# Graph attention on Trainium2: one of ten scaled one-hot copies moved from ScalarE into a fused VectorE maximum

## The reference, cut to what matters

```python
h = x @ Wn.T + bn
e = edge_attr @ We.T + be
a = leaky_relu(sum((h[src] + e) * attn, axis=-1), 0.01)
m = segment_max(a, dst, num_segments=N)
a = exp(a - m[dst])
denom = segment_sum(a, dst, num_segments=N)
out = relu(segment_sum(h[src] * (a / (denom[dst] + 1e-16))[..., None], dst, num_segments=N))
```

## Time and profile before

| | |
|---|---|
| median of three runs | 3936.38 us (3935.75 to 3937.24) |
| the profiled execution | 3933.78 us, its span 3932.0 us |
| busy over the span | PE 80%, PEld 59%, DVE 61%, ACT 46%, POOL 31% |
| granted clock, mean of the span | 0.919 |
| mean DMA rate | 167 GB/s |

### The profile page before, as it was taken

The page is one execution under the profiler, slowest core; times in us unless marked ns, Lnnn a source line. Parts: engine busy times, 40 slices in busy tenths (PEclk is TensorE's granted clock), DMA queues, the critical chain, the costliest instruction groups (busy, mean ns, idle before and its releaser), DMA issues. The chain is left out here.

```text
span 3932.0 us, 83459 instructions
## 1 busy us (share of the span) xinstructions
PE 3146.6 (80%) x17737; PEld 2338.0 (59%) x17738; DVE 2408.5 (61%) x6494; ACT 1816.4 (46%) x6302; POOL 1227.2 (31%) x988
## 2 busy tenths in 40 slices
PE   5666666998887776989944445898999899999978
PEld 4444445887876665767733335787888444445455
DVE  7999998987876565234467777777766400001754
ACT  1888883344445552011189985777776000000111
POOL 1688888888888810111000000000000000002512
PEclk9999999999998898999955558999999999999989
DMA  2444444677788884767576654434332643541067
GB/s 98 127 121 122 120 123 109 182 223 222 239 243 267 270 287 152 226 201 212 167 222 213 206 177 131 144 120 127 108 102 70 204 131 120 185 155 56 0 222 260
DMA packets 438469, 654.85 MB, mean 167 GB/s; under 512 B 102637, under 2 KB 293742, under 8 KB 438244
## 3 DMA queue, kind: packets, MB, share of 16 engines
q1 hardware_dynamic: 351298, 519.69, 42.5%
q10 hardware_dynamic: 56434, 125.33, 8.9%
q0 software_dynamic: 30640, 8.64, 3.1%
HBM read 436.96 MB, written 215.57 MB: 166 GB/s over the span
## 5 line engine op out<-in xcount | busy, mean ns | idle before, releaser
L1076 POOL DMA_INDIRECT slots<-all_B,put_index x800 | 1039.2, 1299 | 341.6 <-issue 335.5
L2354 PE MATMUL gio_po<-gio_T,all_A 125*128 125x500 f32 (+1 forms) x1400 | 530.9, 541 | 5.8 <-DMA gio_T<-pair 5.8
L2354 PEld LDWEIGHTS gio_po<-gio_T,all_A 125*128 125x128 f32 x1400 | 250.2, 190 | 283.3 <-issue 276.7
L1047 PE MATMUL put_ps<-put_right_in,put_left_in 128*128 128x125 f32 x2210 | 318.7, 294 | 65.8 <-ACT put_left_in L904 65.3
L2101 PE MATMUL att_ps<-att_right,att_left 128*125 128x125 f32 x2380 | 312.9, 285 | 70.0 <-ACT att_right L2122 56.6
L1337 ACT ACTIVATE lm_raised<-lm_hot,srt_words 128x125 f32<-128x125 bf16 x1200 | 350.9, 385 | 35.8 <-DVE srt_words L1237 24.8
L1655 PE MATMUL c_po<-c_halves,c_T 125*125 125x512 f32 x1250 | 327.7, 411 | 19.7 <-DVE c_halves L1747 10.0
L1371 PE MATMUL lm_ps<-lm_v,lm_node 125*128 x1220 | 170.5, 184 | 215.5 <-issue 79.2
L2101 PEld LDWEIGHTS att_ps<-att_right,att_left 128*125 128x125 f32 x2380 | 284.7, 191 | 94.2 <-issue 84.7
L1047 PEld LDWEIGHTS put_ps<-put_right_in,put_left_in 128*128 128x128 f32 x2210 | 281.0, 202 | 89.8 <-ACT put_left_in L904 75.6
L2175 DVE SCALAR_TENSOR_TENSOR att_power<-soft_negated,srt_words,att_far 128x125 f32 (+1 forms) x1190 | 320.1, 344 | 3.7 <-ACT att_right L2122 3.3
(11 more groups left out here) (441 smaller groups left out, 5245.3 us busy)
## 6 DMA issues: line engine op xcount, KB each, us to landing
c_T<-counts SPq DMA_DIRECT2D x255, 312.5 KB, 3.4
pair<-put_T ACTq DMA_DIRECT2D x125, 625.0 KB
att_ring<-hot SPq DMA_DIRECT2D x480, 160.0 KB
gio_T<-pair SPq DMA_DIRECT2D x60, 1250.0 KB, 5.8
hot<-put_hot SPq DMA_DIRECT2D x448, 160.0 KB
all_A<-in_edge_attr_dram SPq DMA_DIRECT2D x100, 448.0 KB
lm_planes<-src_rows SPq DMA_DIRECT2D x123, 320.0 KB, 3.9
counts<-put_T ACTq DMA_DIRECT2D x125, 312.5 KB
```

What stands on the lines that cost most here:

```text
L1047: ins = t_.matmul(tile(1, c), left_in[:, c, :], right_in[:, c, :], start=False, stop=False, skip_group_check=True)
L1076: nc.gpsimd.indirect_dma_start(slots, bass.IndirectOffsetOnAxis(index[:, C * g + j:C * g + j + 1], 0), stage[:, C * g + j, :], None).then_ ...
L2354: ins = t_.matmul(po[:, i % 2, h, 0:w], A[:, b, 128 * h:128 * h + 128], tiles, start=(b == 0), stop=(b == NB - 1))
```

## The change

ScalarE makes nine copies instead of ten. The halving becomes two VectorE instructions: a maximum over four pairs of copies (500 columns), and one `scalar_tensor_tensor` that multiplies the tenth one-hot, read from the ring `hot`, by its logit and takes the maximum with the fifth copy (125 columns). As VectorE now reads `hot`, SyncE waits for `grouped >= g+1` before it loads the ring's next slot. Apart from that, VectorE's block loop reads the two bounds of a block with one load of two registers (`Bounds`), where two loads of one register stood.

```diff
+class Bounds:
+    def __init__(self, eng, nc, s, k, name):
+        self.eng, self.nc, self.table = eng, nc, k["group_start"]
+        self.regs = s.registers(eng, name)
+
+    def at(self, d, n=0):
+        regs = self.regs[2 * n:2 * n + 2]
+        self.eng.load(regs, self.table[0:1, ds(d, 2)])
+        first, past = (self.eng.snap(r, donate=True) for r in regs)
+        return self.nc.s_assert_within(first, 0, NG - 1), self.nc.s_assert_within(past, 1, NG)
...
                         sp.wait_ge(lifted, g + 1)
                         sp.sem_inc(passed, 1)
+                        sp.wait_ge(grouped, g + 1)
+                        sp.sem_inc(passed, 1)
                         if not last or j < 3:
                             load_hot(g + 1, j + 1)
                         sp.wait_ge(hot_landed[j], 32 * i + 32)
...
-                    v.tensor_tensor((top if first else pairs)[:, :], lift[:, 0:G // 2 * P], lift[:, G // 2 * P:G * P], ALU.max
-                                    ).then_inc(grouped, 1)
+                    into, q = (top if first else pairs)[:, :], G // 2 - 1
+                    v.tensor_tensor(into[:, 0:q * P], lift[:, 0:q * P], lift[:, (q + 1) * P:(G - 1) * P], ALU.max)
+                    v.scalar_tensor_tensor(into[:, q * P:q * P + P],
+                                           hot[:, ds(g % RING, 1), :].rearrange("p a n -> p (a n)")[:, (G - 1) * S:(G - 1) * S + P],
+                                           logit[:, ds(G * g + G - 1, 1)], lift[:, q * P:q * P + P], ALU.mult, ALU.max
+                                           ).then_inc(grouped, 1)
...
+                bounds = Bounds(dve, nc, s, k, "bound")
                 with dve.Fori(0, NB) as d:
-                    g0, g1 = group_range(dve, k, d)
+                    g0, g1 = bounds.at(d)
...
-                        for c in range(G):
+                        for c in range(G - 1):
                             ins = nc.scalar.activation(raised[:, j % 2, c * P:(c + 1) * P], hot[:, j, c * S:c * S + P], ACT.Copy,
                                                        scale=logit[:, ds(G * g + c, 1)])
```

## The result

The changed kernel takes **3967.55 us** (median of four runs, 3965.67 to 3974.66) against 3936.07 (median of four, 3931.81 to 3937.24): ratio 1.008, 95% interval 1.0065 to 1.0095, **+31.5 us**. The prediction had the direction, half of the size (+14), and an upper end (3966) that the median passes by 1.5 us.

A forecast was written before the change was run, and what follows sets the result against it. It took ScalarE's copies to bound the 379 us stretch, the round through VectorE close behind. SyncE's later release (+15 us) and the block changes (-1) gave +14 on the median 3936.4, so 3950.4 us; range 3932 to 3966.

The forecast's parts named there:

- `grouped` after the halving's start: On VectorE, with the halving split in two instructions, `grouped` was to come 0.94 us after the halving starts, 0.13 later.
- SyncE's road: From the halving's end through SyncE's wait, loads and transfers to ScalarE's copy: 1.96 to 2.05 us, against 1.56 through the logits.
- ScalarE's idle time: Expected to rise to some 60 us, put down to SyncE's increment of `hot_arrived` in nearly every group, not to the logits.
- the prediction's own signs: What would show it right, among them ScalarE's busy time falling by 35 us while the stretch grows from 379 to some 393.
- Landings: Arrival of SyncE's one-hot transfers: 3.4 us free against a median landing of 2.5; late ones could add 0 to 4 us.
- SyncE's own turn allows it: SyncE's time from one pair of transfers to the next, 2.89 us, was held to fit under the new 3.02 a group.
- `Bounds` was mis-sized: One load of both bounds on VectorE was to save 0 to 0.52 us per change of block, taken as 0.35.
- the other round: Of two interleaved rounds of groups, a block change costs one 1.18 us, the other 0.77, as nine copies can catch up.
- The rest of the program does not touch the changed lines, so the whole argument lies in these 379 us: Only the stretch from 1976 to 2355 us, where ScalarE's copies run, was considered; no term covered later stages.
- Rival 1: SyncE's added wait costs nothing and the logits' round rules: -17 us, so 3919 us; chance 13%.
- the changes of block: At 24 places where VectorE starts a new block, 0.35 us each was to be saved: 8 us if the wait cost nothing.
- The slack of 0.04: Over two groups, ScalarE's own 5.80 us and the round through VectorE, 5.76, were only 0.04 us apart.

## Why the prediction was right in direction and half in size

**The mechanism holds.** ScalarE had no slack, the added wait put the release of group g behind halving g-2, and what stands behind the wait on SyncE decides: two instructions more behind it gave +8.3 us (6.2 more than the same two in front of it), one transfer fewer -26.6, the wait for the right group -23.8, and the wait alone was enough for +30.9. Single terms:

- `grouped` after the halving's start: predicted 0.94, measured 0.940 (0.811 before). The halving of 500 columns takes 0.680, 0.13 less; the fused instruction 0.344, as in the earlier trace rows; the overlap is 0.08. The rule for fp32 `tensor_tensor` that the prediction weighed (the Trainium skill, VectorE: DVE Perf Modes, "The TRN2 errata") gives an estimate of 0.678 for 500 columns, and the trace agrees with 0.680. Taken for the 125 columns of the fused operation the estimate would be 0.29, and the trace has 0.344; the sum with the measured row was the better one.
- SyncE's road: first transfer 0.84 predicted, 0.83 to 0.86 where SyncE came in time; pair 0.85; the copy 0.25 to 0.36 behind it. Where SyncE is in time this is the 1.96 to 2.05 of the prediction.
- ScalarE's idle time was expected at some 60 us and put down to SyncE; it is 87, and for all but one group it is SyncE's. The 60 didn't fit the prediction's own signs: 35 us less busy in a stage 14 us longer make 49 more, on top of the 36 of before. Measured are 28 less busy (a run of copies that ends in idle time shows its last copy in full, so not every copy saved is 0.29) and 23 longer. Halvings alternate between 2.5 and 3.5 us where 2.8 and 3.2 were expected.
- Landings: late by over 0.1 us in 6 turns, 2.4 us in all, inside the 0 to 4 that was allowed.
- One slip in the sum: 3.02 against 2.90 is 0.12 a group and 14.3 us, and not 0.125 and 15.

**The step that failed** is "SyncE's own turn allows it". It compared SyncE's turn of 2.89, read in one slot of the loop, with the mean pitch of 3.02. But the pitch isn't even: two rounds are interleaved, the change of block pushes them apart, and halvings 2.53 us apart give SyncE less than the 2.6 to 2.7 of its shortest turn. Nor are SyncE's turns alike. The one that goes round the loop takes at least 3.14, more than the mean itself, and the trace of before had it at 3.04 with nothing waited for:

```profile
2153.77 0.85 SPq L1179 DMA_DIRECT2D lm_hot<-hot  x2
...
2156.81 0.85 SPq L1179 DMA_DIRECT2D lm_hot<-hot  x2
```

So SyncE comes late in 32 of 117 turns. The mean road from the halving's end to the copy is 2.12 us (increment 1.90, and 0.22 from it to the copy) against 1.98, the mean of the predicted 1.96 in three slots and 2.05 in one: 0.14 x 117 / 2 = 8 us at most, of the 9 that are missing between +14 and +23.

**`Bounds` was mis-sized.** The prediction put one load of two registers on VectorE between 0.31, one register, and 0.47, SyncE's load of two. It takes 0.526. From the end of the logits over the reduction to the next halving it is now 2.00 us in the median (2160.97 to 2162.98 in the timeline) against 2.20, a saving of 0.20 in place of 0.35: 0.15 x 24 = 3.6 us less. These two together could be 12, more than the 9; some of it must fall where the other round had room. That share wasn't measured.

**A whole term was missing**: the 7 us of the attention stage. "The rest of the program does not touch the changed lines, so the whole argument lies in these 379 us" was wrong by 7.1 of 31.5 us. Nothing in the trace of before pointed to it. Without it the +23.2 would have given about 3959, inside the range.

**Rival 1 had the wrong price.** With the wait out of the way it forecast -17: 9 us from ScalarE's shorter turn, 8 from the changes of block. With the right wait and one register value the stage gains 4.4, and `Bounds` alone gains 4.9. So the 9 are 0, and the 8 are 5. Of the 0.29 us of the tenth copy, 0.26 turn into ScalarE's idle time in the usual group (median over the groups), and the waits put it down to the logits, 43.6 us in 61 places against 24.8 in 24. They come through VectorE, whose step carries the fused instruction now; that this is the reason was argued from the round and not tried by itself. The slack of 0.04 that the prediction read from the timeline was the right warning, and it should have been held against this rival's gain too.

## What to carry to other kernels

A wait added to a queue costs what stands behind it: count everything between the wait and the increment that another engine needs, put in front of the wait whatever doesn't need it, and let it name the very group that last read the slot; here either repair took away the whole loss in the stage. Hold a queue's longest turn, the one round its loop included, against the shortest interval between the events it waits for, and not one turn against the mean. And when a total moves by a few tenths of a per cent, compare the lengths of the untouched stages as well: the same kernel with seven idle instructions in it was 6.6 us slower in a later one.

## What the runs showed of the hardware that was not expected

- The place of a loop in VectorE's program changed its time: 657.3 to 658.7 us at index 1211 to 1213, 663.9 to 664.6 at 1216 to 1220, with the same instructions and durations. The Trainium skill (Runtime: NRT & Kernel Launch, "Instruction fetch mechanics") says that a taken branch whose target isn't in the instruction buffer has to fetch it first. No run here shows a fetch, so this remains a candidate.
- A load of two registers on VectorE takes 0.526 us against two of 0.31; SyncE's took 0.47. Joining two loads saves 0.09 us in loads, and 0.20 in all with the register work.
- A turn of SyncE that goes round its loop took 0.42 us more than its neighbours between `hot_arrived` and the next wait (0.49 against 0.07).
- One register value made behind a satisfied wait, where another stands ready, delays ScalarE's copy by 0.073 us.
- Idle time behind waits for three semaphores was put down to the logits for 30 to 43 us, though in 118 of 119 groups the first copy followed SyncE's increment.
